# The loading and preparation of weights moved from a stage of its own into the edge sort of a four-layer graph network

## The reference

```
x = layernorm(x + gatv2(x, edges, W_l, b_l, W_r, b_r, att, bias, gamma, beta))   # softmax over edges by target
x = layernorm(x + edge_attention(x, edges, kernel, kernel_attention))            # clipped exp scores
x = layernorm(x + dot_attention(x, edges, query, key, kernel, biases))           # 8 heads, softmax by source
x = layernorm(x + relational(x, rel_emb, deg ** -0.5, Wn, Wl, Wa, edges, types)) # 2 layers
```

## Time and profile before

| | us |
|---|---|
| median of 3 runs | 7950.01 |
| lowest, highest | 7939.81, 7964.99 |
| profiled execution | 7932.62 |
| its span in the trace | 7930.9 |

### The profile page before, as it was taken

One profiled execution on the slowest core, in us unless ns is written; L12 is line 12 of the kernel. 1 busy time (PEld: TensorE's weight loads), 2 busy tenths in 40 slices (PEclk: granted clock), 3 DMA queues, 4 the chain that ended last, 5 costly groups with the idle time before them and its releaser, 6 DMA issues. The chain is left out here.

```text
span 7930.9 us, 112131 instructions
## 1 busy us (share of the span) xinstructions
PE 4807.8 (61%) x32954; PEld 3931.4 (50%) x32954; DVE 4479.6 (56%) x15028; ACT 2093.2 (26%) x4735; POOL 5513.5 (70%) x5311
## 2 busy tenths in 40 slices
PE   3699888566666647777756556554555556444442
PEld 2366665455655536666635555553444444333332
DVE  8999999577777653333346666665444443211113
ACT  8455444122222241111121111112232223111110
POOL 0377777577777557777747777774777774677775
PEclk9999999788888855555566777776555558555555
DMA  0022221566666436666546777762555553333333
GB/s 21 20 56 56 53 53 41 139 162 160 162 161 160 117 79 135 135 135 135 131 134 203 205 207 206 205 200 65 156 156 155 156 156 89 97 105 105 104 105 80
DMA packets 1304014, 990.39 MB, mean 125 GB/s; under 512 B 287713, under 2 KB 1192995, under 8 KB 1303411
## 3 DMA queue, kind: packets, MB, share of 16 engines
q0 software_dynamic: 183088, 352.33, 17.9%
q1 hardware_dynamic: 700995, 378.63, 17.1%
q10 hardware_dynamic: 419328, 252.26, 11.7%
HBM read 613.75 MB, written 368.79 MB: 124 GB/s over the span
## 5 line engine op out<-in xcount | busy, mean ns | idle before, releaser
L997 POOL DMA_INDIRECT l_rows<-tab,by_src x1664 | 1802.6, 1083 | 615.3 <-issue 506.6
L997 POOL DMA_INDIRECT l_rows<-tab,by_dst x832 | 976.3, 1173 | 324.0 <-issue 236.2
L997 POOL DMA_INDIRECT l3a_rows<-tab,by_dst x832 | 803.6, 966 | 297.7 <-issue 252.9
L997 POOL DMA_INDIRECT l3b_rows<-tab,by_dst x832 | 793.0, 953 | 294.4 <-issue 253.2
L715 POOL DMA_INDIRECT sorted_dst<-pay,place_i x783 | 792.2, 1012 | 275.3 <-issue 237.8
L1143 PE MATMUL l_ps_z<-l_win,l_sel_t 128*128 128x128 f32 x3328 | 747.2, 351 | 213.3 <-DMA l_rows<-tab,by_dst 187.0
L1444 PE MATMUL l3b_ps_o<-l3b_rows,l3b_sel 128*128 128x128 f32 x1664 | 425.7, 437 | 630.5 <-DMA l3b_rows<-tab,by_dst 630.5
L1143 PEld LDWEIGHTS l_ps_z<-l_win,l_sel_t 128*128 128x128 f32 x3328 | 601.6, 248 | 236.9 <-issue 183.1
L1444 PEld LDWEIGHTS l3b_ps_o<-l3b_rows,l3b_sel 128*128 128x128 f32 x1664 | 370.5, 328 | 686.0 <-issue 686.0
L1444 PE MATMUL l3a_ps_o<-l3a_rows,l3a_sel 128*128 128x128 f32 x1664 | 404.1, 419 | 480.2 <-DMA l3a_rows<-tab,by_dst 480.2
L1471 DVE TENSOR_SCALAR l3b_sel<-iota,by_dst 128x128 f32<-128x128 f16 x832 | 185.6, 302 | 859.4 <-PE l3b_ps_o L1444 855.9
(11 more groups left out here) (423 smaller groups left out, 12331.0 us busy)
## 6 DMA issues: line engine op xcount, KB each, us to landing
parts<-l_sums ACTq DMA_DIRECT2D x416, 264.0 KB
l_win<-win SPq DMA_DIRECT2D x1664, 64.0 KB
parts<-l3a_sums SPq DMA_DIRECT2D x208, 512.0 KB, 3.0
l_row<-slot_rows ACTq DMA_DIRECT2D x624, 128.0 KB, 3.2
parts<-l_sums ACTq DMA_DIRECT2D x208, 272.0 KB
parts<-l3b_sums SPq DMA_DIRECT2D x208, 256.0 KB
low_bc<-lo_rows SPq DMA_DIRECT2D x194, 256.0 KB
l_rows<-tab,by_src POOLq DMA_INDIRECT x1664
```

Source lines behind the costliest of these rows:

```text
L997: pool.indirect_dma_start(rows[:, q, g, :], None, table, bass.IndirectOffsetOnAxis(ap=index[:, k * G + g:k * G + g + 1], axis=0))\
```

## The change

The stage for weights is gone. Its instructions stand in `sort_edges`:

- POOL clears w1 and one_rows behind its other clears at the start of the sort; it clears zero_rows after it has waited for all counts.
- DVE clears rel_w as its second instruction.
- SP, behind the first four fetches, waits for `made` 8, for all counts and for POOL's clears, then issues the 24 loads and 3 pads, and goes on with the runs and the other fetches.
- behind the main loop and the permutation PE does its transposes and products, DVE the splitting of the biases and the copies; then they go on with the tail of the sort.
- SP, ahead of its wait for the scatters, waits for the splitting, sends the three bias pieces and waits for them.

The small buffers are now views into `ent` (biases and pieces) and `low` (transposed kernel, zero rows, attention columns, relation rows), and PSUM banks 4 and 5 take the products.

```
+            sp.wait_ge(made, 8)
+            sp.wait_ge(counted, 2 * US)
+            sp.wait_ge(w_cleared, 3)
+            for to, of in loads:
+                sp.dma_start(to, of).then_inc(w_loaded, 16)
+            for table, width in pads:
+                sp.dma_start(table[NP:NW, :], zero_rows[:, 0:width]).then_inc(w_loaded, 16)
             for i, k in enumerate(KEYS):
                 sp.wait_ge(started, 3 * i + 3)
...
             for k in KEYS:
                 sp.wait_ge(turned_lo[k], US)
+            sp.wait_ge(w_split, 9)
+            for i in range(3):
+                sp.dma_start(c.bias_rows[i:i + 1, :], pieces[:, i]).then_inc(w_pieces_in, 16)
+            sp.wait_ge(w_pieces_in, 48)
             sp.wait_ge(self_sent, 16 * NT)
...
+            pe.wait_ge(w_loaded, w_all)
+            pe.wait_ge(mult_done, len(units))
+            pe.transpose(ps_t, c.w1[:, 0:D], c.ident[:]).then_inc(w_turned, 1)
...
             pe.wait_ge(back_in, 16)
...
             dve.memset(zero_nt[:], 0.0).then_inc(prep, 1)
+            dve.memset(c.rel_w[:], 0.0).then_inc(rel_zero, 1)
...
             for u in range(len(units) + 4):
                 tick(u)
 
+            dve.wait_ge(w_loaded, w_all)
+            dve.tensor_tensor(bias_rest[:, 0:D], bias_rest[:, 0:D], bias0, ALU.add).then_inc(w_split, 1)
...
+            dve.wait_ge(w_split, 2)
+            for i in range(3):
+                dve.tensor_copy(pieces[:, i], bias_rest).then_inc(w_split, 1)
+                if i < 2:
+                    dve.wait_ge(w_split, 3 + 3 * i)
+                    dve.tensor_copy(bias_back, pieces[:, i]).then_inc(w_split, 1)
...
+            dve.tensor_copy(c.w1[:, D:D + 2], ps_a)
             dve.wait_ge(code_done, 1)
...
+            pool.memset(c.w1[:], 0.0).then_inc(w_cleared, 1)
+            pool.memset(c.one_rows[:], 1.0).then_inc(w_cleared, 1)
+            pool.wait_ge(counted, 2 * US)
+            pool.memset(zero_rows, 0.0).then_inc(w_cleared, 1)
             pool.wait_ge(begun, 1)
...
-        constants(nc, c)
-        load_weights(nc, c, weights)
-        sort_edges(nc, c, src, dst, etype, lo_rows, sorted_dst, runs, etype_at)
+        constants(nc, c)
+        sort_edges(nc, c, weights, src, dst, etype, lo_rows, sorted_dst, runs, etype_at)
```

More of the change, by code:

```diff
@@ L135, in _, with sort_edges @@
             dve.tensor_copy(c.ident16[:], c.ident[:]).then_inc(cst_cast, 1)
-def sort_edges(nc, c, src, dst, etype, lo_rows, sorted_dst, runs, etype_at):
+def sort_edges(nc, c, w, src, dst, etype, lo_rows, sorted_dst, runs, etype_at):
     KEYS = (DST, SRC)
@@ L212, in sort_edges @@
         zeroed = kit.sem("sort_zeroed")
+        w_cleared, w_loaded, w_turned, w_copied, w_split, w_pieces_in = (
+            kit.sem(f"w_{n}") for n in ("cleared", "loaded", "turned", "copied", "split", "pieces_in"))
+        rel_zero = kit.sem("w_rel_zero")
         stepped, steps_in, steps_out, rises_done, above_done = (
@@ L215, in sort_edges @@
         *sent, self_sent = c.pool_dma[0:5]
+        bias_at = ent[:].rearrange("p f t -> p (f t)")
+        bias_f, bias_h = bias_at.bitcast(F32), bias_at.bitcast(BF16)
+        bias_rest, bias_back, bias0 = bias_f[0:1, 0:5 * D], bias_f[0:1, 5 * D:10 * D], bias_f[0:1, 10 * D:11 * D]
+        pieces = bias_h[0:1, 22 * D:37 * D].rearrange("p (i d) -> p i d", i=3)
+        free = low[:].rearrange("p k t -> p (k t)")
+        kernel_t, zero_rows, att_cols = free[:, 0:P], free[:, P:P + D], free[:, 2 * P + 2 * D:2 * P + 2 * D + 2]
+        rel_rows = free[0:RELS // 2, 3 * P + 2 * D:3 * P + 4 * D].rearrange("p (h d) -> p h d", h=2)
+        rel_t = free[:, 3 * P + 4 * D:3 * P + 4 * D + RELS]
+        ps_t, ps_a = bank[4][:, 0:P], bank[4][:, 0:2]
+        ps_rt, ps_rw = bank[5][:, 0:RELS], bank[5].rearrange("p (h l d) -> p h l d", h=2, l=2)
         block = st.enter_context(nc.Block())
@@ L222, in col @@
             return NT + s * UG + g
+        row = lambda a: a.rearrange("(a n) -> a n", a=1)
+        spread = lambda a: row(a).to_broadcast([P, D])
+        loads = [(c.w0[:, 0:D], w["L0_gnn_W_l"]), (c.w0[:, D:2 * D], w["L0_gnn_W_r"]),
+                 (bias_rest[:, 0:D], row(w["L0_gnn_b_l"])), (bias_rest[:, D:2 * D], row(w["L0_gnn_b_r"])),
+                 (c.w1[:, 0:D], w["L1_gnn_kernel"]),
+                 (c.w2[:, 0:D], w["L2_gnn_key_kernel"]), (c.w2[:, D:2 * D], w["L2_gnn_kernel"]),
+                 (c.w2[:, 2 * D:], w["L2_gnn_query_kernel"]),
+                 (bias_rest[:, 2 * D:3 * D], row(w["L2_gnn_key_bias"])),
+                 (bias_rest[:, 3 * D:4 * D], row(w["L2_gnn_bias"])),
+                 (bias_rest[:, 4 * D:], row(w["L2_gnn_query_bias"])), (bias0, row(w["L0_gnn_bias"])),
+                 (c.gamma[:], spread(w["L0_gnn_gamma"])), (c.beta[:], spread(w["L0_gnn_beta"])),
+                 (c.att[:], spread(w["L0_gnn_att"].rearrange("h c -> (h c)"))),
+                 (att_cols[:, 0:1], w["L1_gnn_kernel_attention"][D:2 * D, :]),
+                 (att_cols[:, 1:2], w["L1_gnn_kernel_attention"][0:D, :])]
+        for l in range(2):
+            loads += [(c.w3[:, l, 0:D], w["L3_gnn_Wn"][l]), (c.w3[:, l, D:2 * D], w["L3_gnn_Wl"][l]),
+                      (c.w3[:, l, 2 * D:], w["L3_gnn_Wa"][l])]
+        loads.append((rel_rows, w["L3_gnn_rel_emb"].rearrange("(h r) d -> r h d", h=2)))
+        pads = [(c.win0, D), (c.win1, 4), (c.win2, D)]
+        w_all = 16 * (len(loads) + len(pads))
         units = [(k, s) for s in range(US) for k in KEYS]
@@ L411, in _ @@
                 permute((u - 5) // 2, (u - 1) % 2)
+            pe.wait_ge(w_loaded, w_all)
+            pe.wait_ge(mult_done, len(units))
+            pe.transpose(ps_t, c.w1[:, 0:D], c.ident[:]).then_inc(w_turned, 1)
+            for h in range(2):
+                mm = pe.transpose(ps_rt[:, h * (RELS // 2):(h + 1) * (RELS // 2)], rel_rows[:, h],
+                                  c.ident[0:RELS // 2, 0:RELS // 2])
+            mm.then_inc(w_turned, 1)
+            pe.wait_ge(w_copied, 1)
+            pe.matmul(ps_a, kernel_t, att_cols, start=True, stop=True).then_inc(w_turned, 1)
+            pe.wait_ge(w_copied, 2)
+            for h, (r0, r1) in enumerate(((0, P), (P, RELS))):
+                for l in range(2):
+                    mm = pe.matmul(ps_rw[0:r1 - r0, h, l], rel_t[:, r0:r1], c.w3[:, l, 0:D], start=True, stop=True)
+            mm.then_inc(w_turned, 1)
             pe.wait_ge(back_in, 16)
@@ L675, in _ @@
                 tick(u)
+            dve.wait_ge(w_loaded, w_all)
+            dve.tensor_tensor(bias_rest[:, 0:D], bias_rest[:, 0:D], bias0, ALU.add).then_inc(w_split, 1)
+            dve.tensor_tensor(bias_rest[:, D:2 * D], bias_rest[:, D:2 * D], bias0, ALU.subtract).then_inc(w_split, 1)
+            dve.wait_ge(w_split, 2)
[4 more added lines that the diff above has]
+                    dve.tensor_copy(bias_back, pieces[:, i]).then_inc(w_split, 1)
+                    dve.wait_ge(w_split, 4 + 3 * i)
+                    dve.tensor_tensor(bias_rest, bias_rest, bias_back, ALU.subtract).then_inc(w_split, 1)
+                    dve.wait_ge(w_split, 5 + 3 * i)
+            dve.wait_ge(w_turned, 1)
+            dve.tensor_copy(kernel_t, ps_t).then_inc(w_copied, 1)
+            dve.wait_ge(w_turned, 2)
+            dve.tensor_copy(rel_t, ps_rt).then_inc(w_copied, 1)
+            dve.wait_ge(w_turned, 4)
+            dve.wait_ge(rel_zero, 1)
+            dve.tensor_copy(c.rel_w[:, 0], ps_rw[:, 0])
+            dve.tensor_copy(c.rel_w[0:RELS - P, 1], ps_rw[0:RELS - P, 1])
+            dve.tensor_copy(c.w1[:, D:D + 2], ps_a)
             dve.wait_ge(code_done, 1)
@@ L717, in _ @@
                         pay[:, col(s, g), :], None).then_inc(sent[s % 4], 16)
[L720 to L818, removed]
```

## The result

| | before | after |
|---|---|---|
| median of 7 runs each | 7939.58 us | 7910.39 us |
| lowest, highest | 7931.34, 7964.99 | 7902.67, 7922.55 |
| span of the profiled execution | 7930.9 | 7912.9 |

The ratio is 0.9961, 95% interval [0.9951, 0.9971]: 31 us less, between 23 and 39. Forecast: 7926 us in a range of 7908 to 7946, ratio 0.9970. The measured time lies in the range, and the forecast's ratio at the upper end of the interval. The forecast started from 7950.01, the median of three runs; over seven runs the kernel before took 7939.58, from which the expected 23.6 us less would give 7916.

A forecast was written before the change was run, and what follows sets the result against it. POOL, issuing without a gap in the long loops, was taken to set the time, plus stretches where it has nothing to do. 24.07 us less at the start, 0.5 lost at the sort's end: 7950.01 to 7926 us, range 7908 to 7946.

The forecast's parts named there:

- Start: Program start: the sort's entry comes behind the constants' barrier instead of the weights' one, 24.07 us earlier; added clears cost 0.
- The doubt about the first transfer: Program start: the sort's loads, now the first DMAs, might take 0.7 us more or less; taken as 0.
- Middle: Middle of the sort: 11.5 us of SP's queue and a 0.20 us POOL clear, hidden under waits, cost 0.
- The 2 us for POOL's issues beside the loads: Self-edge scatters: 0.2 us more for each of some nine issues beside the loads, hidden under a 36.9 us wait.
- End of the sort: Behind the main loop: preparation of 8.37 us and bias DMAs, covered by 21.8 us on SP, make nothing late.
- POOL beside DVE: Sort's last scatters: DVE's preparation beside them lengthens them, between 0.3 and 1.7 us; 0.5 us taken.
- Rival (a): End of the sort: POOL is locked out for the length of each cast, 2.4 us, giving 7928 us; 10%.
- the rule of the Trainium skill: End of the sort: GpSimd's DMA issue waits for DVE's whole 2-port copy or cast; five casts add at most 2.4 us.
- Sum: Whole kernel: 24.07 - 0 - 0.5 = 23.6 us less, passed on undiminished, from a median of 7950.01 to 7926 us.
- Rival (b): End of the sort: the preparation becomes the last to end, so the wait is only moved, 7950 us; 1%.
- Rival (c): TensorE's clock: halved in load step, 7959 us (6%); halved in 6540 to 6760, 8017 us (4%); decides at grant 0.62.
- Rival (d): Program start: code fetch or a cold first transfer is merely uncovered, 2 to 5 us, giving 7930 us; 9%.

The follow-up runs named there:

- e9: The kernel before with no edit, executed once for its trace on the 7940 us chip: main loop 1030 us, span 7938.8 us.
- e2: The kernel before with its weights stage run twice in a row, on the slow chip: ratio 1.0023 [1.0001, 1.0044] to the kernel before.
- e3: The changed kernel with the old weights stage put back ahead of the sort, on the slow chip: ratio 1.0003 [0.9986, 1.0020] to the kernel before.
- e7: The changed kernel with 250 more DMAs of 64 KB behind the mid-sort loads and pads, slow chip, trace only: first main-loop scatter 38.1 us later than e1's.
- e12: The changed kernel with 60 chained copies ahead of the bias splitting, 7940 us chip, trace only: read-back at 1400.75 us, 14.1 us later than without them.
- e10: The changed kernel with SP's wait for the split and the three bias DMAs behind the read-back: ratio 0.9966 [0.9954, 0.9978] to the kernel before.
- e11: The changed kernel once more, no edit, on the 7940 us chip: 7916.07 against 7939.64 us, ratio 0.9970 [0.9960, 0.9979] to the kernel before.
- e1: The changed kernel again, no edit, on the slow chip: medians 9171 against 9191 us, ratio 0.9997 [0.9977, 1.0018] to the kernel before.
- e8: The changed kernel with an empty stage between constants and sort, slow chip, trace only: sort's first POOL instruction at 4.45 us instead of 3.56.

## Why the prediction was right, by its steps

- Start: 24.07 us expected, 24.06 measured, and 24.18 for the first mask. Against e9, where the sort begins at 27.22, it is 23.66, and the stages of e2 and e3 cost 23.6 and 23.5. The doubt about the first transfer was void.
- Middle: 0 expected and found. The cover was read as 76 us and is 73; e7 shows that the row of the wait is the right measure. The 2 us for POOL's issues beside the loads were not there even under cover: the 49 scatters took 51.6 us before and 51.5 after.
- End of the sort: nothing late, as expected. Cover 21.8 us expected, 22.6 by e12. The preparation took 8.46 us for an expected 8.37.
- POOL beside DVE: 0.5 us taken. The longer scatters of the first trace add to 0.27 (1.14 and 1.07 against 0.97) and one of 1.21 beside the subtraction, which the kernel before has too (1.30). The traces of e10 and e11 have the same three. From first to last scatter the pair agrees: 1029.6 us before, 1029.7 after. Rival (a), and with it the rule of the Trainium skill ("SBUF — State Buffer", section "SBUF: two separate sides") in the form in which I used it, fails here: the five casts together cost 0.27 us at most and not 2.4, and 43 copies beside POOL didn't lengthen one scatter. The section also says that whichever starts first gets the ports for its instruction and the other blocks. DVE's 0.637 against 0.516 us from copy to copy agrees with that in kind and not in size: DVE loses some 0.24 us per scatter, which takes 0.97.
- Sum: 23.6 expected; 23.6 in e11, 29.2 between the medians of the first comparison. Of the 16.0 us between the forecast's 7926.4 and the measured 7910.4, 10.4 come from the three runs it started from and 5.6 from the gain. The range had room for both; the steps at the start and the end of the sort are what the traces confirm.
- Rival (b), given 1%: it did not happen where I predicted, and it is what happens on the other chip. The step that was too narrow is its bound: I worked out how much longer the preparation would have to be, with POOL's end given. But the cover is POOL's end minus DVE's, and it went from 22.6 us to below zero because the main loop slowed, not the preparation. The change is then worth about 17 us of 9191 (23.5 to 24.1 for the stage, less 6.7), by estimate a ratio of 0.998, which the interval of e1 holds but does not show.
- Rival (c): in the load step's 54 us the grant is 0.87 after the change (1399 to 1453) and 0.88 before (1423 to 1477). In the later node step it is 0.82 for the same products in both (6540 to 6766 before, 6522 to 6747 after), far from the 0.62 that would have decided. On the slow chip PE decides in the sort's main loop, and for both kernels alike; what decides in its later stages is not shown.
- Rival (d): e8 and the start's rows leave no room for it.

## What to carry to other kernels

A stage between barriers is worth its whole length when all its work fits under waits that already exist; read the wait of each queue that gets new work, and take it as the cover (113.2 us read and 113.0 found in the middle, 23.5 read and 22.6 found at the end). A cover at the end of a loop is the difference between the engine that sets the pace and the ones that do the added work, so it lasts only while the pace stays with that engine: say what the order of their ends is, and put the added DMAs behind the transfer that the next step waits for. Seven runs of each kernel told a gain of 24 us in 7940 from none, but not 24 us from 31, and on the slow chip twelve runs told nothing; the timeline shows at once which stage has moved.

## What the runs showed of the hardware that I had not expected

- One and the same kernel took 7940 us on one chip and 9191 on another, 16% more. Of the 1224 us between the first trace of the changed kernel and e1, 527 lie in the sort's main loop, 40 ahead of it, 6 at the end of the sort and 651 behind the first gather. In the main loop the grant is 0.84 against 0.98, and PE, ACT and DVE pause without a releaser, PE for up to 8.8 us and most of all. What makes them pause is open, and so is what slows the later stages.
- Chained copies of 1 x 640 float32 on DVE followed each other after 0.637 us while POOL issued indirect DMAs beside them, and after 0.516 in the same run once POOL was done; the scatters stayed at 0.97 us.
- Of 250 DMAs of 64 KB in a row on SP's queue, 201 took 0.47 us from start to start, as the weights' loads of that size do (0.43 and a gap of 0.04). The other 48 steps took 1.24 us in the mean, most of them between 262 and 319 us of the trace, while POOL scattered the self edges until 312.5. What holds them is open.
